# A gated attention and feed-forward block on one Trainium2 core: the third gating cycle regrouped and in three passes, and ACT making the high parts of four late splits

## What is computed

```python
def _coupling_net(h, w1, b1, w2, b2, w3, b3, w4, b4):
    h = _gelu(h @ w1 + b1)
    h = _gelu(h @ w2 + b2)
    h = _gelu(h @ w3 + b3)
    return jax.nn.sigmoid(h @ w4 + b4)
def _twist(x):
    o_r, o_i, p_r, p_i = jnp.split(x, 4, axis=-1)
    return jnp.concatenate([p_r, -p_i, -o_r, o_i], axis=-1)
...
    out = x
    for _ in range(NUM_CYCLES):
        tf = _coupling_net(out, ...)
        combined = 0.7 * gf + 0.3 * tf
        coupling = BASE_COUPLING + adaptive_range * (combined - 0.5) * 2.0
        out = out + coupling * _twist(out)
    return out
...
x = x + jnp.tanh(g_ffn[0]) * _L0_ffn_ref(_layernorm(x, axis=-1), ...)
```

## Time and profile before

| | us |
|---|---|
| median of three runs | 1733.85 |
| the profiled execution's own time | 1734.33 |
| its span | 1732.5 |
| PE busy | 1703.2 |
| DVE busy | 1443.0 |
| ACT busy | 1237.3 |
| POOL busy | 660.4 |

### The profile page before, as it was taken

The page is one execution under the profiler, slowest core; times in us unless marked ns, Lnnn a source line. Parts: engine busy times, 40 slices in busy tenths (PEclk is TensorE's granted clock), DMA queues, the critical chain, the costliest instruction groups (busy, mean ns, idle before and its releaser), DMA issues. The chain is left out here.

```text
span 1732.5 us, 34074 instructions
## 1 busy us (share of the span) xinstructions
PE 1703.2 (98%) x12392; PEld 1282.1 (74%) x12392; DVE 1443.0 (83%) x2554; ACT 1237.3 (71%) x2169; POOL 660.4 (38%) x590
## 2 busy tenths in 40 slices
PE   8999999999999999999999999999999999999997
PEld 7888888777777777777777777777775675774873
DVE  6554545999999999999999999999678976968868
ACT  4222224999999999999999999999664374365454
POOL 3432342423278552587432875543235010100100
PEclk9999999999999999999999999999999999999999
DMA  7777675765468665567764676555503514222101
GB/s 279 274 246 284 234 268 153 190 183 135 138 162 191 132 150 123 136 212 142 160 152 118 183 172 134 136 110 152 165 11 93 168 50 122 89 74 49 64 1 49
DMA packets 160951, 254.70 MB, mean 147 GB/s; under 512 B 25488, under 2 KB 77968, under 8 KB 160800
## 3 DMA queue, kind: packets, MB, share of 16 engines
q1 hardware_dynamic: 110416, 158.84, 29.1%
q0 software_dynamic: 49808, 92.82, 23.8%
q10 hardware_dynamic: 576, 1.05, 0.2%
HBM read 168.47 MB, written 84.18 MB: 146 GB/s over the span
## 5 line engine op out<-in xcount | busy, mean ns | idle before, releaser
L1021 DVE CUSTOM_DVE_ANT_0 a_neg<-a_sc_ps,am 128x1024 f32<-128x1024 f32 x512 | 622.0, 1215 | 1.4 <-PE a_sc_ps L853 1.3
L961 ACT ACTIVATE a_prob<-a_neg,a_row_min 128x1024 f32<-128x1024 f32 x512 | 586.2, 1145 | 13.5 <-DVE a_row_min L1021 7.8
L867 PEld LDWEIGHTS a_tr_ps<-ident,a_prob 128*128 128x128 f32 x4096 | 461.2, 140 | 89.3 <-issue 53.4
L867 PE MATMUL a_tr_ps<-ident,a_prob 128*128 128x128 f32 x4096 | 519.8, 274 | 0.9 <-ACT a_probT L939 0.9
L996 DVE COPY a_probT<-a_tr_ps 128x512 f32<-128x512 f32 x512 | 350.7, 685 | 37.4 <-PE a_tr_ps L867 36.0
L939 ACT ACTIVATE a_probT<-a_tr_ps 128x512 f32<-128x512 f32 x512 | 304.4, 595 | 35.4 <-PE a_tr_ps L867 15.9
L749 POOL DMA_DIRECT2D a_q_st<-q_parts x144 | 79.6, 558 | 195.6 <-PE a_sc_ps L853 159.7
L853 PE MATMUL a_sc_ps<-k_first,a_q_st 96*128 96x512 f32 x384 | 126.5, 427 | 0.1
L853 PE MATMUL a_sc_ps<-a_k_st,a_q_st 96*128 96x512 f32 x384 | 126.2, 427 | 0.0
L887 PE MATMUL a_o_ps<-a_probT,a_v 128*32 128x256 f32 x2048 | 123.6, 382 | 0.6 <-ACT a_o L950 0.6
L887 PE MATMUL a_o_ps<-a_probT,v_first 128*32 128x256 f32 x2048 | 123.8, 382 | 0.0
(11 more groups left out here) (223 smaller groups left out, 3140.8 us busy)
## 6 DMA issues: line engine op xcount, KB each, us to landing
a_q_st<-q_parts POOLq DMA_DIRECT2D x144, 128.0 KB, 3.8
k_first<-k_parts POOLq DMA_DIRECT2D x24, 512.0 KB, 7.9
a_k_st<-k_parts POOLq DMA_DIRECT2D x24, 512.0 KB, 8.3
a_m_raw<-mask SPq DMA_DIRECT2D x24, 512.0 KB, 5.2
a_adj_raw<-adj SPq DMA_DIRECT2D x24, 512.0 KB, 6.2
k_parts<-p_out_hi SPq DMA_DIRECT2D x32, 256.0 KB, 4.4
k_parts<-p_out_lo SPq DMA_DIRECT2D x32, 256.0 KB, 6.6
v_all<-p_v_out SPq DMA_DIRECT2D x8, 1024.0 KB, 4.4
```

What stands on the lines that cost most here:

```text
L867: last = pe.transpose(tr_ps[:, bank(u, half), j * P:(j + 1) * P], prob[:, r % NPROB, t * P:(t + 1) * P], ident[:])
L961: act.activation(prob[:, r % NPROB, :], neg[:, r % 2, :], ACT.Exp, scale=-1.0, bias=row_min[:, r % 2:r % 2 + 1], accum_out=row_sum[:, r // ...
L1021: dve.tensor_tensor_reduce(out=neg[:, r % 2, :], in0=sc_ps[:, r % 2, :], in1=am[:, 2 * qb + qt, :], scale=-1.0, scalar=3.4e38, op0=ALU.add ...
```

## The change

Third cycle regrouped. The mix of cycle 2 is written as u + c (B - beta A), where u = A + beta B is the mix of cycle 1. So u is kept: the h1 of cycle 1 goes to buffers of its own (`h1_second`), which lie where the second half's attention parts X1 are. B - beta A is made in place by DVE (`turned`), in pieces at k = 0, 1 and 2. After the second coupling there are one product and one sum per tile (`third_cycle`). The scaling of both couplings by range and base is a second ACT operation in `gate`.

Third cycle in three passes. ACT makes h1 twice (`u_hi_third` in the same buffers), DVE makes the low part, and PE takes a copy of the split w2 (`w2_kept`), which POOL starts as a transfer from SBUF to SBUF once the first layer is done, since the split w2 lies where the first half's parts of the next batch are loaded. Those loads wait for the copy, and the second half's loads wait for the end of layer 2 of k = 5, no longer for the end of the first layer.

Late splits. For n = 28 to 31 POOL does the product and the low part alone (`split_late`), and ACT makes the high part by one copy (`high_late`), behind h2 of steps k = 0 to 3. The copy of w2 is started between the third and the fourth.

Also two of the four `finish` of half 0 have their twisted product made by ACT at k = 5 (`twist`) and added by DVE, and the columns need three small operations more since beta and c are sent as they are.

```diff
@@ -139,6 +139,20 @@
...
+def split_late(pool, w, n):
+    pool.wait_ge(w.loaded, 80 * (n + 1))
+    pool.tensor_tensor(w.o[:], w.o[:], w.rinv[:], ALU.mult).then_inc(w.step, 1)
+    pool.wait_ge(w.step, 5 * n + 4)
+    pool.tensor_tensor(w.lo[:], w.o[:], w.hi[:], ALU.subtract).then_inc(w.step, 1)
+def high_late(act, w, n):
+    act.wait_ge(w.stored, 32 * n)
+    act.wait_ge(w.step, 5 * n + 1)
+    act.activation(w.hi[:].bitcast(F32R), w.o[:], ACT.Copy).then_inc(w.step, 3)
...
@@ -1072,8 +1086,11 @@
...
+        w2_kept = [nc.alloc_sbuf_tensor_at(f"f_w2_kept{part}", [P, ET, F2], F32R, offset=sb.offset + 4096 * part) for part in range(2)]
...
+        h1_second = [nc.alloc_sbuf_tensor_at(f"f_h1_second{j}", [P, ET, CH], F32, offset=SB_AM + 8192 * j) for j in range(NJ)]
+        u_hi_third = [nc.alloc_sbuf_tensor_at(f"f_u_hi_third{j}", [P, ET, CH], F32R, offset=SB_AM + 8192 * j) for j in range(NJ)]
...
@@ -1255,12 +1269,18 @@
...
+            def keep_w2(b):
+                pool.wait_ge(product_ready, 4 * ET * NJ * (b + 1))
+                pool.wait_ge(w2_lo_ready, b + 1)
+                for kept, tile in zip(w2_kept, (w2_hi, w2_lo)):
+                    pool.dma_start(kept[:], tile[:]).then_inc(w2_kept_loaded, 16)
...
-                    pool.wait_ge(z2_ready, 2 * turn(b - 1, SPLIT - 1, 1) + 2)
+                    pool.wait_ge(z2_ready, 2 * turn(b - 1, 0, 1) + 2)
+                    pool.wait_ge(w2_kept_loaded, 32 * b)
...
-                    pool.wait_ge(product_ready, 4 * ET * (NJ * (b - 1) + j + 1))
+                    pool.wait_ge(z2_ready, 2 * turn(b - 1, CYCLES - 1, 1) + 2)
...
@@ -1292,10 +1312,13 @@
...
-                    for n in range(LATE, 2 * B * GPB):
-                        split_weighted(pool, weighted, n)
+                    for n in range(LATE, 2 * B * GPB - 1):
+                        split_late(pool, weighted, n)
+                keep_w2(b)
+                if first:
+                    split_late(pool, weighted, 2 * B * GPB - 1)
...
-                    for j in (1, 0):
+                    for j in range(NJ):
...
@@ -1373,20 +1396,24 @@
...
+                if n in SPLIT:
+                    pe.wait_ge(w2_lo_ready, b + 1)
+                    if n:
+                        pe.wait_ge(w2_kept_loaded, 32 * (b + 1))
+                w_hi, w_lo = w2_kept if n else (w2_hi, w2_lo)
+                high = u_hi_third[j] if n else u_hi[j]
...
+                        if n in SPLIT:
+                            last = three_pass(pe, acc[:, 2 * j + m, :], w_hi[:, t, ms], w_lo[:, t, ms], high[:, t, :], u_lo[j][:, t, :],
...
-                        last = pe.matmul(acc[:, 2 * j + m, :], w2[:, t, m * P:(m + 1) * P], u[j][:, t, :], start=t == 0, stop=t == ET - 1)
+                        else:
+                            last = pe.matmul(acc[:, 2 * j + m, :], w2[:, t, ms], h1_second[j][:, t, :], start=t == 0, stop=t == ET - 1)
...
@@ -1511,9 +1538,15 @@
...
+                if n == 1:
+                    act.wait_ge(product_ready, 4 * ET * NJ * (b + 1))
+                elif m == 0:
+                    act.wait_ge(z2_ready, 2 * turn(b, 1, j) + 2)
...
-                if n < SPLIT:
-                    act.activation(u_hi[j][:, m, :], u[j][:, m, :], ACT.Gelu, bias=small.b1[:, m:m + 1])
+                if n == 1:
+                    act.activation(h1_second[j][:, m, :], u[j][:, m, :], ACT.Gelu, bias=small.b1[:, m:m + 1]).then_inc(h1_ready, 1)
+                    return
+                act.activation(u_hi_third[j][:, m, :], u[j][:, m, :], ACT.Gelu, bias=small.b1[:, m:m + 1])
...
@@ -1527,7 +1560,12 @@
...
-                act.activation(coef[:, j, :], z4[:, j, :], ACT.Tanh, scale=0.5, bias=small.half_b4[:]).then_inc(t_ready, 1)
+                if n == 0:
+                    wait(act, rows_stored, 32 * NJ * b)
+                act.activation(coef[:, j, :], z4[:, j, :], ACT.Tanh, scale=0.5, bias=small.half_b4[:]).then_inc(tanh_ready, 1)
+                act.wait_ge(base_ready, b + 1)
+                act.wait_ge(tanh_ready, NJ * ((CYCLES - 1) * b + n) + j + 1)
+                act.activation((beta if n == 0 else coef)[:, j, :], coef[:, j, :], ACT.Identity, scale=small.range_3[:], bias=base[:]).then_inc(t_ready, 1)
...
@@ -1581,23 +1619,38 @@
...
+                    def next_h1(*tiles):
+                        if between:
+                            for m in tiles:
+                                h1(*other, m)
+                    if k == 3:
+                        next_h1(0)
...
+                    if first and k < 2 * B * GPB - LATE:
+                        high_late(act, weighted, LATE + k)
...
-                    if between:
-                        h1(*other, 0)
+                    if k == 5:
+                        twist(b, 0, 2)
+                    next_h1(1 if k == 3 else 0)
...
-                    if between:
-                        h1(*other, 1)
+                    if k == 5:
+                        twist(b, 0, 3)
+                    if k < 3:
+                        next_h1(1, 2)
+                        gate(b, n, j)
+                        next_h1(3)
+                        continue
+                    if k == 4:
+                        next_h1(1)
+                    next_h1(2, 3)
...
-                    if between:
-                        h1(*other, 2)
-                        h1(*other, 3)
...
@@ -1664,58 +1717,71 @@
...
+            def split_u(b, n, j, tiles=range(ET)):
+                for m in tiles:
...
-                    dve.tensor_tensor(u_lo[j][:, m, :], u[j][:, m, :], u_hi[j][:, m, :].bitcast(F32), ALU.subtract).then_inc(u_lo_ready, 1)
...
+                    dve.tensor_tensor(u_lo[j][:, m, :], u[j][:, m, :], (u_hi_third if n else u_hi)[j][:, m, :].bitcast(F32), ALU.subtract).then_inc(u_lo_ready, 1)
+            def in_turn(first, second):
+                first(0)
+                for m in range(1, ET):
+                    first(m)
+                    second(m - 1)
+                second(ET - 1)
+            def second_cycle(b, j):
+                k = ET * (NJ * b + j)
+                dve.wait_ge(t_ready, turn(b, 0, j) + 1)
+                def scale(m):
+                    dve.tensor_tensor(u[j][:, m, :], Bt[j][:, m, :], beta[:, j, :], ALU.mult).then_inc(mul_ready, 1)
...
+                    dve.tensor_tensor(u[j][:, m, :], u[j][:, m, :], A[j][:, m, :], ALU.add).then_inc(u_ready, 1)
+                in_turn(scale, add)
+            def turned(b, j, tiles):
+                k = ET * (NJ * b + j)
+                dve.wait_ge(u_ready, ET * ((CYCLES - 1) * b * NJ + j + 1))
+                for m in tiles:
+                    dve.tensor_tensor(A[j][:, m, :], A[j][:, m, :], beta[:, j, :], ALU.mult).then_inc(twist_step, 1)
+                    if m > tiles[0]:
+                        subtract(j, m - 1, k)
+                subtract(j, tiles[-1], k)
+            def subtract(j, m, k):
+                dve.wait_ge(twist_step, k + m + 1)
+                dve.tensor_tensor(Bt[j][:, m, :], Bt[j][:, m, :], A[j][:, m, :], ALU.subtract).then_inc(turned_ready, 1)
+            def third_cycle(b, j):
+                k = ET * (NJ * b + j)
+                dve.wait_ge(t_ready, turn(b, 1, j) + 1)
+                dve.wait_ge(turned_ready, k + ET)
+                def scale(m):
+                    dve.tensor_tensor(Bt[j][:, m, :], Bt[j][:, m, :], coef[:, j, :], ALU.mult).then_inc(B_scaled, 1)
+                def add(m):
+                    dve.wait_ge(B_scaled, k + m + 1)
+                    dve.tensor_tensor(u[j][:, m, :], u[j][:, m, :], Bt[j][:, m, :], ALU.add).then_inc(u_ready, 1)
+                in_turn(scale, add)
...
+                be, c, al, both = raw_cols[:, j, 0], raw_cols[:, j, 1], cols[:, j, 0], cols[:, j, 1]
...
-                dve.tensor_scalar(cols[:, j], raw_cols[:, j], small.gate_f[:], None, ALU.mult).then_inc(cols_ready, 1)
+                dve.scalar_tensor_tensor(al, be, -1.0, c, ALU.mult, ALU.mult).then_inc(cols_step, 1)
+                dve.tensor_tensor(both, be, c, ALU.add).then_inc(cols_step, 1)
+                dve.wait_ge(cols_step, 2 * k + 2)
+                dve.tensor_scalar(al, al, 1.0, small.gate_f[:], ALU.add, ALU.mult).then_inc(cols_ready, 1)
+                dve.tensor_scalar(both, both, small.gate_f[:], None, ALU.mult).then_inc(cols_ready, 1)
...
@@ -1798,17 +1864,30 @@
...
-                    if n < CYCLES - 1:
-                        coefficients(b, n, j)
-                        mix(b, n + 1, j)
-                        if n + 1 < SPLIT:
-                            split_u(b, n + 1, j)
+                    if n == 0:
+                        second_cycle(b, j)
+                        turned(b, 0, ((0, 1, 2), (3,))[j])
+                        if j:
+                            turned(b, 1, (0, 1))
+                    elif n == 1:
+                        third_cycle(b, j)
+                        split_u(b, 2, j, (0,))
+                        if j == 0:
+                            turned(b, 1, (2,))
```

(12 more changed lines are left out.)

82 lines of the change are left out of this document (21 added, 61 removed).

## The result

The changed kernel takes 1746.72 us (median, 1743.51 to 1749.86), the kernel before 1733.88: ratio 1.0074, 95% interval 1.0062 to 1.0087. The forecast was 1734.7 us, range 1728 to 1739.5, with 0.23 for slower. It was wrong.

The account below looks back on a forecast made before the run. PE, busy 1703.2 of 1732.5 us, was taken as the bound. First batch +1.5, inner changes -1.0 and end +0.4 gave +0.9: 1735.2 us, or 1734.7 by the median; range 1728 to 1739.5.

Parts of the forecast that it names:

- The timetable of the late batch: Late batch, steps 0 to 5: DVE and ACT operand times, with PE stalling 1.8 us for step 5's low part.
- Of 2.6 us about 0.55 is left: Late batch: PE's third-cycle saving of 2.6 us per batch shrinks to about 0.55 because operands come late.
- The change between inner batches: Undisturbed batch changes: DVE is 0.6 us later, inside its 1.70 us, so PE's 0.5 passes on.
- the term of -1.0: Two changes between undisturbed batches, each passing on PE's 0.5 us: -1.0 us in all.
- The tail: End of the last batch: DVE busy 0.3 us longer with half 0, small operations in front: +0.4 us.
- What goes: First batch: POOL's slowing of DVE, and so PE's wait before its first layer 3, disappears: -2.1 us.
- What comes: First batch: POOL's six operations beside steps 0 to 3 cost DVE 4.2 us, bounded 0 to 10.
- The round of part to part: First batch: copy, POOL's work, store and reload take 9.3 us per late part, 10.8 with the longest reload.
- up to 0.9 us: First batch: waiting on ACT because late-part rounds of 9.3 us exceed steps of 8.46 to 9.63.
- rival 3: First batch: POOL blocks DVE wholly, six times 1.59 us, 3.1 us more: +4.0, 1737.8 us; chance 0.07.
- Rival 2: First batch: ACT's in-order copies wait for late parts, delaying h3, PE and columns: +4.7, 1738.5 us; chance 0.13.
- The columns "at about 1362": First batch: DVE gets the gate's columns at about 1362 on before's clock, 1.5 us late.

Follow-up runs that it names:

- the float32 kernel: The changed kernel with ACT's four copies moved to later-safe places and the third cycle's layer 2 in float32 as before, still regrouped: 1731.79 us, ratio 0.9986.

## Why the prediction was wrong, step by step

- *The timetable of the late batch: right in its places, 0.6 us too short.* The stall for the low part was 1.74 us (1.8 forecast), the wait for h2 0.47 (0.3), step 3-4 8.60 (8.45). From the last stall to step 5's layer 3 it was 6.74 us where I had 6.5. These small terms eat the 0.55 us that the forecast left. "Of 2.6 us about 0.55 is left" is 0.0; the runs without low parts and without the second activation show that DVE's row takes most of it.
- *The change between inner batches: right.* 71.46 against 71.44; DVE's 0.6 us more are inside its slack, and the late load of half 1 made nobody wait. Since PE had gained nothing before it, there was nothing to pass on: the term of -1.0 was +0.1.
- *The tail: right sign, half the size.* +0.87 against +0.4. I had taken the four small operations as 0.3 of work; they are 0.53 and stand in the way whole, with DVE's later end of half 0 in front.
- *"What goes", -2.1: right.* No wait before the first layer 3.
- *"What comes": the step that failed.* The sum has +1.5 us for the first batch, bounded by +5; it was +11.2 (13.3 in the table less the 2.1 of "what goes"). The round of part to part was 0.6 + 1.6 + 5.7 + 1.4, with 1.4 us for POOL's product. I let POOL's operations cost DVE 1.06 us each and never asked what DVE's row costs POOL. The product took 4.93 and 3.12 us; the copies waited 1.16, 3.08 and 2.90 us where "up to 0.9 us" was forecast for the round, and PE 6.8 us in three stalls behind them (1.10, 3.20, 2.54), plus the slower clock. What the forecast did price came nearly as it said: five operations of DVE took 1.64 to 1.76 us instead of 0.69, some 5.1 us in all where it had 6.4, so rival 3 fell. The page of the Trainium skill that I weighed, SBUF — State Buffer, "Who interferes with whom", says that the order of issue decides which of the two waits. I used it with DVE as the loser alone (my rival 3). It would not have given the size either: six operations of DVE that began after the product of 1332.60 went ahead of it, so here the measurement is against the rule. Writes in place of POOL's two operations took the long steps away, and so did other places for the copies, which shows the cause.
- *Rival 2 was nearest, for another reason.* Its place was right (copies in order, in front of h3), also that the columns are late with it. Its cause was not, or only in part: the reloads ahead of the second and third product were 5.87 and 5.89 us, like the short ones before (the kernel before has 5.71, 5.34 and 7.16; the forecast read only the first and the last). The reload ahead of the fourth product was long, 8.20 us, but with writes it was 7.86 and PE's 2.54 us became 0.28. With products of 1.3 us ACT's wait for the third part would be gone and that for the fourth 1.1 us instead of 2.90, an estimate from the rows. Only the first of the three stalls, 1.10 us, is mainly the round's: its product did not starve. Its price of 4.7 us was a third of what came.
- *The columns "at about 1362": 1373.08.* Of the 11 us, 2.65 are the later start of the phase, the last part left POOL at 1354.3 instead of 1346.5, of which these are a part, and the landing of the rows behind 4 MB took 8.3 us where I had 6.5. (The forecast's own terms, 1.5 less 0.9 plus 0.6, make 1.2 and not 1.5; this changes nothing.) Then the wait passed on: ACT's products for half 0, new in front of h3, waited 2.64 us for what DVE makes of the columns (their row is above), and PE 3.18 for that h3, 0.78 before. The forecast counted the columns' lateness once, for DVE, and not that the change had put ACT and so PE behind it.

What stays open: how much of the first batch's 13.3 us is the clock alone. No run had the stalls without it. By the windows it is at most 6.9 us, an estimate: the five windows below full clock (the four above and 0.87 for 1335 to 1340) lack 6.9 us of it together, and PE was not busy throughout them.

## What to carry to other kernels

When work of one engine is cut and given to another in order, price the wait for its slowest supplier in both directions: here a POOL product late in an unbroken row of DVE's two-input operations took two to four times as long, and everything behind ACT's copy paid. Put such a helper where its operand has long been ready; that gave back the 12 us here (1746.7 to 1734.6). And where a faster form of a matmul needs operands from the vector engines, use it for the part whose operands fall in their gaps (half 0, 0.55 us a batch) and not for the part at the end of their row.

## What the runs showed of the hardware

- POOL and DVE, two-input operations on SBUF at the same time: POOL products within DVE's row took 4.93, 3.12, 4.28 and 4.22 us instead of 1.3, while DVE's operations followed each other at 0.60; one that began 0.09 us ahead of DVE's operation took 1.29, and DVE's 1.76. A fill by POOL took 0.53 us within the row.
- When a product starves: in all traces of this case together, the 23 products that began during a DVE operation and up to 3.1 us after DVE's last pause took 1.29 to 1.86 us. The 13 that began 3.6 us after it or later took 3.04 to 5.48, and each got in at DVE's next pause, which was 0.03 to 0.04 us long. Why the place in the row matters no run shows.
- After or around PE waits of 2.5 to 3.2 us the granted clock over 5 us was 0.62 to 0.79, and four matmuls of 1.98 us took 3.54.
- Gate rows of 2 KB took 8.3 us to land behind four loads of 1 MB (8.2 in the float32 kernel), and 13.39 behind six (12.9 in before with the late splits).
